# Attention key sums on one core: a DMA adds the second pair of key tiles to the first, and GpSimd issues transfers of its own

## The reference

```python
xn = layernorm(x)
q, k, v = heads(xn @ Wq.T), heads(xn @ Wk.T), heads(xn @ Wv.T)      # 16 heads of 32
diff = max(|q|^2 + |k|^2 - 2 q.k, 0)
cosh = 1 + 2 * diff / max((1 - |q|^2) * (1 - |k|^2), 1e-6)
attn = softmax(-arccosh(cosh))
a = (attn @ v) @ Wo.T
f = xn @ int4(kernel) + bias + (xn @ lora_a) @ lora_b
out = x + a + f
```

## Time and profile before

| | |
|---|---|
| median of 3 runs | 2296.81 us (2295.22 to 2297.49) |
| the profiled execution's own time | 2304.41 us |
| its span, first to last instruction | 2302.6 us |
| TensorE busy | 2188.5 us, 95% |
| VectorE busy | 2083.3 us, 90% |
| ScalarE busy | 2074.9 us, 90% |
| GpSimd busy | 324.1 us, 14% |
| TensorE clock granted | 0.991 of full speed, on average |

### The profile page before, as it was taken

How to read it: one execution, slowest core, us unless ns; L and a number is a source line. 1 busy time by engine, 2 the same in 40 slices (tenths; PEclk the granted TensorE clock), 3 DMA queues, 4 the chain that set the end, 5 groups by cost and what they waited for, 6 DMA issues and landing times.

```text
span 2302.6 us, 45880 instructions
## 1 busy us (share of the span) xinstructions
PE 2188.5 (95%) x17416; PEld 863.9 (38%) x17416; DVE 2083.3 (90%) x2798; ACT 2074.9 (90%) x1907; POOL 324.1 (14%) x199
## 2 busy tenths in 40 slices
PE   6889889999999999999999999999999999989897
PEld 3433333444344343444333433333333334333232
DVE  6789889999999999999998999999899999889897
ACT  4499999999999999999999998999999999989893
POOL 0010001111111111111111111111111111111021
PEclk9999999999999999999999999999999999999999
DMA  5544325554345553544555453555434555354342
GB/s 183 174 115 111 103 79 156 151 157 137 113 140 159 158 158 113 165 129 130 169 151 164 112 143 120 162 150 166 127 109 143 155 150 147 111 160 127 102 145 89
DMA packets 373400, 318.62 MB, mean 138 GB/s; under 512 B 83085, under 2 KB 296221, under 8 KB 373177
## 3 DMA queue, kind: packets, MB, share of 16 engines
q1 hardware_dynamic: 372680, 314.06, 47.2%
q0 software_dynamic: 496, 1.60, 0.2%
HBM read 176.55 MB, written 138.13 MB: 137 GB/s over the span
## 4 chain that ended last, share of the span: by engine, by line
PE 56%; ACT 19%; DVE 12%; issue 10%; SPq 1%; DMA 1%; DVEq 0%; ACTq 0%; POOL 0%
PE pM L320 21%; PE pU L240 12%; PE pO L252 12%; ACT root L565 8%; ACT root L571 8%; PE pZ L268 6%; DVE root L908 3%; DVE root L903 2%; PE pM L310 2%; ACT qk L592 2%; PE pM L293 1%; DVE kx L779 1%; PE pM L296 1%; DVE xn L737 1%; ACT o_s L577 0%
## 5 line engine op out<-in xcount | busy, mean ns | idle before, releaser
L565 ACT ACTIVATE root<-pU 128x1024 f32<-128x1024 f32 x1008 | 1017.3, 1038 | 87.2 <-PE pU L240 83.2
L571 ACT ACTIVATE root<-root 128x2048 f32<-128x2048 f32 x512 | 988.4, 1931 | 54.3 <-DVE root L903 54.3
L903 DVE TENSOR_SCALAR root<-root 128x2048 f32<-128x2048 f32 (+1 forms) x512 | 650.5, 1270 | 71.6 <-ACT root L565 71.6
L240 PE MATMUL pU<-QS,KS 100*128 100x512 f16 x2048 | 614.3, 382 | 35.7 <-ACT root L565 27.4
L908 DVE TENSOR_TENSOR root<-root 128x2048 f32<-128x2048 f32 x256 | 582.9, 2277 | 2.1 <-ACT root L571 2.0
L252 PE MATMUL pO<-root,VX 128*32 128x512 f32 x4096 | 501.5, 604 | 7.4 <-DVE o_s L893 4.5
L1076 POOL TENSOR_TENSOR sqr<-qk 128x512 f32<-128x512 f32 x112 | 206.4, 1843 | 1143.9 <-ACT qk L592 1057.9
L240 PEld LDWEIGHTS pU<-QS,KS 100*128 100x128 f16 x2048 | 177.1, 98 | 377.0 <-issue 143.3
L268 PE MATMUL pZ<-root,ones 128*32 128x512 f32 x2048 | 268.6, 596 | 16.6 <-DVE root L908 16.6
L252 PEld LDWEIGHTS pO<-root,VX 128*32 128x32 f32 x4096 | 104.8, 109 | 278.3 <-issue 196.4
L320 PE MATMUL pM<-Wqh,xT 128*128 128x512 f16 x512 | 172.9, 383 | 12.1 <-DVE xT L742 7.4
(11 more groups left out here) (188 smaller groups left out, 2219.1 us busy)
## 6 DMA issues: line engine op xcount, KB each, us to landing
v_d<-v_o SPq DMA_DIRECT2D x64, 264.0 KB, 2.1
k_d<-kx SPq DMA_DIRECT2D x64, 264.0 KB, 2.1
KT<-k_d SPq DMA_DIRECT2D x64, 264.0 KB
VX<-v_d SPq DMA_DIRECT2D x64, 264.0 KB
xts<-in_x SPq DMA_DIRECT2D x32, 512.0 KB, 4.7
xT_d<-xT SPq DMA_DIRECT2D x64, 256.0 KB, 2.0
QS<-qh_d SPq DMA_DIRECT2D x128, 128.0 KB
KS<-kh_d SPq DMA_DIRECT2D x128, 128.0 KB
```

The source lines that it names most:

```text
L240: mm = pe.matmul(pU[:, col:col + HALF], KS[i][:, h, j * P:(j + 1) * P], QS[i][:, h, half * HALF:(half + 1) * HALF], start=True, stop=True)
L565: act.activation(root[:, q % RING, cols], pU[:, cols], ACT.Square).then_inc(squared, 1)
L571: act.activation(root[:, q % RING, :], root[:, q % RING, :], ACT.Sqrt).then_inc(rooted, 1)
L903: v.tensor_scalar(root[:, q % RING, cols], root[:, q % RING, cols], CS * CS, CS * CS, ALU.max, ALU.subtract).then_inc(clamped, 1)
```

## The change

1. **Held sums.** In periods 8 to 55 (`HELD`), `add_pair` of j = 1 writes its result into a new array `held` instead of into `root`. The sum of the second pair (j = 2 and 3) is then added to `held` by a DMA with an accumulate, 1 MB, issued by GpSimd (`accumulate`). `sum_one` does nothing at j = 1 and j = 3; at j = 5 it first sums `held`, after a wait for the DMA, and then its own pair. There are three groups of matmuls by ones instead of four.
2. **Slots.** Even quads use slots 0 to 3 of `root`, odd ones 4 to 6; the waits for a free slot (`wait_free`) are written for each case.
3. **KV.** GpSimd issues the six DMAs of kvl (`pass_kv_low`), SP the ten of kvh, each counted apart.
4. **Waits apart.** KT and VX have semaphores of their own; `distances` waits for QS and KS only, `sum_v` and `key_sums` for the values.
5. **Divide.** `raw`, `rzb`, `ah` and `al` hold one row tile instead of two: `load_raw` and `divide` run in each period with arrays half the size. `out_o` has one buffer. The last pair but one of tiles is divided in arrays borrowed from `held` and KT (`divide_pair`).
6. **Order on SP.** `load_raw` is at step 11 (even) or 12 (odd); where a block is completed, `store_feat` now comes ahead of `load_raw` at step 14.

```diff
+        HELD = range(LEAD, LATE)
+        def slot(q):
+            return 4 + q // 2 % 3 if q % 2 else q // 2 % 4
+        def wait_free(engine, q):
+            u = q - 6 if q % 2 else q - 8
+            if u < 0:
+                return
+            p, j = u // JC, u % JC
+            if j % 2:
+                engine.wait_ge(pair_added, u // 2 + 1)
+                engine.wait_ge(v_summed, u + 1)
+            elif p not in HELD or j >= 4:
+                engine.wait_ge(summed_up, u + 2)
+            elif j == 0:
+                engine.wait_ge(pair_added, u // 2 + 1)
+            else:
+                engine.wait_ge(accumulated, 16 * (p - HELD[0] + 1))
...
             def sum_one(q):
                 p, j = q // JC, q % JC
+                first = j == (JC - 3 if p in HELD else 1)
+                if p in HELD and j < JC - 3:
+                    return
                 pe.wait_ge(pair_added, q // 2 + 1)
...
+                if p in HELD and first:
+                    pe.wait_ge(accumulated, 16 * (p - HELD[0] + 1))
+                    for h in range(G4):
+                        pe.matmul(pZ[h * HD:(h + 1) * HD, :], ones[:, :], held[:, h * HALF:(h + 1) * HALF], start=True, stop=False)
...
             def divide(n):
-                v.wait_ge(raw_loaded, (n // 2 + 1) * 5 * 16)
+                v.wait_ge(raw_loaded, (n + 1) * 5 * 16)
...
             def add_pair(q):
                 v.wait_ge(rooted, q + 1)
                 v.wait_ge(v_summed, q)
+                even = root[:, slot(q - 1), :]
+                into = even
+                if q // JC in HELD and q % JC == 1:
+                    v.wait_ge(summed_up, q // JC * JC)
+                    into = held[:, :]
+                v.tensor_tensor(into, even, root[:, slot(q), :], ALU.add).then_inc(pair_added, 1)
...
                 if o >= 0:
-                    if even and k == 3:
+                    if k == 3:
                         divide(o)
...
+            def accumulate(p):
+                q = p * JC + 3
+                g.wait_ge(pair_added, q // 2 + 1)
+                g.dma_start(held[:, :], root[:, slot(q - 1), :], accum_op=ALU.add).then_inc(accumulated, 16)
+            def pass_kv_low(p):
+                i = p // 2 % 2
+                if p >= 4:
+                    g.wait_ge(summed_up, (p - 2) * JC)
+                g.wait_ge(kv_taken, p // 2 + 1)
+                for h in range(G4):
+                    g.dma_start(KV[i][HD:2 * HD, h, :], kvl[h * HD:(h + 1) * HD, 0:HW]).then_inc(kv_low_loaded[i], 16)
+                for r in (1, 3):
+                    g.dma_start(KV[i][3 * HD + r:3 * HD + r + 1, :, :], kvl[0:P:HD, HW:2 * HW]).then_inc(kv_low_loaded[i], 16)
...
+                if n - LEAD in HELD:
+                    accumulate(n - LEAD)
+                if (n - LEAD) % 2 == 0:
+                    pass_kv_low(n - LEAD)
...
+                if k == (11 if even else 12) and o >= 0 and not last_of_block and p < PERIODS - 1:
+                    load_raw(o + 1, (o + 1) // TPB)
                 if k == 11 and o >= 0:
                     store_out(o)
-                if k == 12 and not even and o >= 0 and not last_of_block and p < PERIODS - 1:
-                    load_raw(o + 1, (o + 1) // TPB)
                 if k == 13 and last_of_block:
                     store_rz((o + 1) // TPB, (o + 1) // TPB)
-                    load_raw(o + 1, (o + 1) // TPB)
...
                 if k == 14 and not even and n < NT:
                     store_feat(n)
+                if k == 14 and last_of_block:
+                    load_raw(o + 1, (o + 1) // TPB)
```

More of the change, by code:

```diff
@@ L137, in fast @@
         W32 = {k: root[:, i, :].rearrange("p (c n) -> p c n", c=KC) for i, k in enumerate("qkv")}
-        W32["o"] = W32["f"] = shares[:, :, :, :].rearrange("p s c n -> p (s c n)").rearrange("p (c n) -> p c n", c=KC)
+        W32["o"] = W32["f"] = held[:, :].rearrange("p (c n) -> p c n", c=KC)
         magnitudes = root[:, 5, :].rearrange("p (c n) -> p c n", c=KC)
-        At, Bl = (a[:, :, :].rearrange("p c n -> p (c n)").bitcast(F32)[0:RANK, :] for a in (ah, al))
+        At, Bl = out_o[0:RANK, :], raw[:, :, :].rearrange("p c n -> p (c n)")[0:RANK, :]
         by_chunk = lambda a: a.rearrange("p (c n) -> p c n", c=KC)
@@ L147, in fast @@
         ah3, al3 = W["v"]
+        raw1, rzb1 = (by_chunk(held[:, i * KC * 2 * P:(i + 1) * KC * 2 * P]) for i in range(2))
+        ah1, al1 = (by_chunk(KT[:, :, :].rearrange("p j n -> p (j n)").bitcast(F16)[:, i * KC * 2 * P:(i + 1) * KC * 2 * P]) for i in range(2))
         raw3 = xts[:, 0:KC - 1, :]
@@ L186, in fast @@
         kv_loaded = [sem("kv_loaded0"), sem("kv_loaded1")]
+        kv_low_loaded = [sem("kv_low_loaded0"), sem("kv_low_loaded1")]
+        values_loaded = [[sem(f"values{i}{h}") for h in range(2)] for i in range(2)]
         stack_loaded = [[sem(f"stack{i}{h}") for h in range(2)] for i in range(2)]
@@ L275, in sum_one @@
                         mm = pe.matmul(pZ[h * HD:(h + 1) * HD, :], kv1[:, h, :], QS[p // 2 % 2][:, h, HALF:N], start=False, stop=True)
-                mm.then_inc(summed_up, 2)
+                mm.then_inc(summed_up, JC - 2 if p in HELD and first else 2)
             def linear(p, bank, part, cols):
@@ L468, in keys @@
                     pe.wait_ge(taken["f"], f_place[m - 1] + 1)
-                pe.wait_ge(stack_loaded[p // 2 % 2][1], (p // 4 + 1) * STACK)
+                for h in range(2):
+                    pe.wait_ge(values_loaded[p // 2 % 2][h], (p // 4 + 1) * VALUES)
                 key_sums(p, 0)
@@ L570, in sinh @@
                     act.wait_ge(multiplied, by_vector.index(2 * q + 1) + 1)
-                act.activation(root[:, q % RING, :], root[:, q % RING, :], ACT.Sqrt).then_inc(rooted, 1)
+                act.activation(root[:, slot(q), :], root[:, slot(q), :], ACT.Sqrt).then_inc(rooted, 1)
             def take_v_sums(p):
@@ L1045, in vector_program @@
             add_pair(QUADS - 1)
-            divide(56)
+            divide_pair()
             divide_last()
@@ L1287, in store_out @@
                 sy.wait_ge(taken["o"], o + 1)
-                sy.dma_start(out[o * P:(o + 1) * P, :], out_o[:, o % 2, :]).then_inc(out_stored[o % 2], 16)
+                sy.dma_start(out[o * P:(o + 1) * P, :], out_o[:, :]).then_inc(out_stored[o % 2], 16)
             def all_stored(n):
```

104 lines of the change are left out of this document (61 added, 43 removed).

## The result

The changed kernel takes 2281.69 us (median of 7 runs, 2275.45 to 2287.91) against 2296.81 before (2295.02 to 2301.99 in 7 runs beside it): ratio 0.9929, 95% interval 0.9917 to 0.9942. That is faster by some 16 us, where 38 were forecast.

What follows compares the result with a forecast made beforehand. PE bounds the kernel, busy 67.15 of 67.76 us per stretch (two periods); 24 stretches at 66.2 save 37.4 us: 2304.41 profiled becomes 2267.0, and the same difference off the 2296.81 median gives 2259. Range 2234 to 2325.

Steps and rivals of the forecast that it cites:

- PE's terms: Steady stretch of two periods: two groups of matmuls by ones (1.94 us) and a 0.61 gap go, 67.76 to 65.21.
- the gap: PE's single idle 0.61 us before `sum_one` of step 11, even period; was to go with that `sum_one`.
- ScalarE's 97%: Steady stretch: ScalarE, busy at most 97.0% as in an early stretch, needs 66.2 us for its 64.23 of work.
- The divide: VectorE: three half-size operations each period, 4.2 us a stretch for 3.9, +0.3; even period relieved of 1.8.
- The accumulate's landing: Accumulating DMA into `held`: lands in 8.7 us, in time for windows of 10.0 (even periods) and 9.6 (odd).
- too late: Rival, 24%: accumulate lands after PE needs `held`, late by 1.8 and 2.2 us (2332) or 3.1 and 3.5 (2394).
- The slots: Waits for free slots of `root` ask only for work PE does before the next `distances` anyway: nothing.
- Nothing, or at most 1 us a stretch: KV in two queues: kvl issued by GpSimd after the accumulate costs nothing, or 1 us if landing behind it.
- Nothing, or a late divide of up to 2 us in 14 places: Order on SP at block ends, `load_raw` behind `store_feat`: no cost, or divide up to 2 us late in 14 places.
- The tail: Periods 56 to 63, like 0 to 7, keep four groups of matmuls by ones: no change in time there.
- It does part of it: Rival, 14%: accumulate late by 1 us in odd periods, or kvl late; stretch near 67.0, -18 us, 2279.
- `linear` waiting for kvl: Sign that the forecast is wrong: the linear matmuls on PE wait for the kvl DMAs; no size given.

## Why the prediction was wrong

*PE's terms: near in sum, one of them misplaced.* The forecast had 1.94 for two groups and 0.61 for the gap, floor 65.21; without a DMA the stretch is 65.52. But the gap goes with the divide alone, four groups kept (66.94 of 66.94 busy); the two groups then take 1.42 (66.94 to 65.52), 0.71 each and not 0.97. The forecast stopped at 66.2 by ScalarE's 97%; it reached 97.5%. It also took one stretch of 67.76 for all 24, 1626 us, where the trace before has 1638.2.

*The divide: its place right, its worth not seen.* The term had a cost of 0.3 us for VectorE and no gain of its own, though it foresaw the relief in the even period. By itself, with the groups by ones unchanged, it takes 0.82 off a stretch (67.77 to 66.95), 24 us in all.

*The accumulate's landing: right.* 8.5 us for 8.7, and 0.95 for its issue. The sums of `held` waited 2.2 us in the whole run. The rival "too late", 24%, did not come. The slots were wrong: they were to ask only "for work that PE does before the next `distances` anyway", and ScalarE waited for the accumulate in 17 places, 13.1 us.

*The step that failed* is the price of that DMA. The sum asked only when it lands, and set its neighbours at "Nothing, or at most 1 us a stretch" (KV) and "Nothing, or a late divide of up to 2 us in 14 places" (shares). What was missing is a term for the load, 5.3 us of packet time on all 16 engines, that each accumulate puts where those need to pass: SP's issues went from 0.59 to 1.40 us where both met, kvl landed after 6.2 us (1.9 in the kernel with no DMA), PE waited 8.2 us for kvh (its weight loads 28.0, in part the same time) and 12.7 for kvl, 6.0 of these after GpSimd's one late issue, and VectorE 33.3 for the shares in 12 places, 2.8 each. Net of what is hidden, 50 us: 0.7 a stretch without a block's end, within the 1 that the forecast allowed for KV and took as nothing, and 3.5 with one, where it allowed 2 for the late divide and took nothing. The Trainium skill (DMA: Bandwidth & Descriptors, section Issuing engines are not separate DMA queues) says that DMAs of all issuers run on the same 16 engines and interleave, and that issuing from several engines saves the sequencer's time alone; the trace agrees, with nothing gained by moving kvl (0.9876 and 0.9875) and SP's copies late behind GpSimd's megabyte. The forecast had the row for it: 94% from 1056 on the earlier trace rows was read for the accumulate's own sake only.

*The tail: wrong.* "Periods 0 to 7 and 56 to 63 keep four groups: nothing there." From the start of period 56 to the end it was 260.0 us before and 244.3 after. Between them stand 255.4 (old divide, no held sums), 252.9 (divide in each period) and 248.2 (kvl on GpSimd too). Each is a single trace, and those of the kernels with held sums have 243 to 249 for nearly the same tail; that it became shorter is seen, and by how much each part did it is not. Which wait went there was not looked into.

*The account.* By ratios, each part on top of the ones before it: slots, waits and order -5, the divide -24, kvl 0, the groups by ones -38 (0.9876 to 0.9711), the accumulates +50. They add up to the measured -16 by the way they are formed, which confirms nothing; what each would be worth in another order was not tried, and each is good to some 3 to 6 us. That the groups' -38 equals the forecast's -38 is luck, since the forecast's had the gap in it and a limit by ScalarE; and the change had two parts more, one for it and one against. The nearest rival was "It does part of it", 2279; its time is right and it names a late kvl, as does the forecast's sign "`linear` waiting for kvl", which came. But kvh and the shares were late too, the accumulate was not late by 1 us in odd periods, and neither kind of stretch has its 67.0 on average (66.4 and 69.6).

What stays open: whether the load on the engines or the longer landing makes the neighbours late, and why SP's issue of a small DMA takes longer beside the accumulate. That it does was seen in the accumulate's and the two copies' traces; what in the path holds it was not tried.

## What to carry to other kernels

A DMA has two prices: when it lands, and how much it loads the engines that all queues share; the second falls on the small transfers with the nearest deadlines, so list these beside each big one and see which have that much room. A big transfer goes behind the small ones of its queue, and not where other queues have their own stores and loads: leaving out 12 of 48 accumulates and turning round two issues gave 26 us. And a part that looks like a helper of the change (here the divide, spread over both periods) is measured by itself: it gave 24 us, and the part in the title, groups and accumulates together, cost 12.

## What was not expected of the hardware

- An accumulate of 1 MB from SBUF to SBUF took 8.5 us to land (7.4 to 10.6) and 5.3 us of packet time on all 16 engines, a copy 5.5 and 2.7.
- SP's issue of a DMA of 2 KB took 0.59 us and, in the timeline above, 1.40 beside an accumulate; 68 of 245 took over 1 us, and 14 of 250 without accumulates.
- GpSimd's issue of 1 MB took 0.95 us, against 0.73 on average for the four of 2 KB behind it.
- After the wait of 9.00 us that ends at 2008.13, the clock granted to TensorE was 0.54 and 0.50 in the two short windows shown with the profile after, the lower level, 1.2 of 2.4 GHz. The engine had been idle since 1999.13. A projection's matmul then took 0.59 us where such matmuls take 0.38 on average: a long wait for a DMA costs more than its own length.
- Beside GpSimd's addition (5.4 us) a VectorE operation on 128x2 took 2.06 us on average, and 0.17 in the kernel with the DMA.
